# Split order of the summed weight blocks and plain fp32 first slices in a 64-sequence LoRA MLP with a per-sequence mix

## The chip, the cores and the metric

One core of one Trainium2 chip runs the kernel. The metric is the device time of one execution in microseconds (us). Before the change the median of 3 runs is 457.58 us (457.47 to 458.84).

## The reference

64 sequences of 32 rows with 512 features (2048 rows of `x`). Each group of sequences picks one of 16 adapters (`itok_B_2_6`) for the first step and one of 16 conditions (`itok_B_0_15`) for the second. All in float32:

```python
def lora_add(base, inp, A, B):
    t = jnp.einsum('bri,bni->bnr', A[0][idx], inp)          # rank 16
    return base + jnp.einsum('bor,bnr->bno', B[0][idx], t) * 0.5
gate = lora_add(x @ W_gate.T, x, A_gate, B_gate)            # 512 -> 1376
up   = lora_add(x @ W_up.T,   x, A_up,   B_up)
act  = silu(gate) * up
x    = x + lora_add(act @ W_down.T, act, A_down, B_down)    # 1376 -> 512
x    = x + einsum('bct,bcd->bdt', x, L1_weights[cond])      # mixes the 32 rows of a sequence
```

## The kernel before, in words

**Tiles and pairs.** Four sequences make a tile of 128 rows, 16 tiles make 8 pairs. The first phase (pairs 0 to 7) computes gate and up, with `xT` (features x rows) as the stationary operand and the weights as the moving one; the result is turned, written to `actT_dram` ("spilled") and read back by the second phase, which runs tile by tile (`down`, 16 times) over 11 chunks of `W_down` and ends each tile with the mix of the tile before it.

**Three products for one.** Every fp32 operand is split into a high fp32r part, copied by ACT (`hi`, L500), and the rest, subtracted by DVE (`lo`, L763; for the adapters' B rows L767). TensorE then runs hi x hi, hi x lo and lo x hi, three matmuls per 128-feature slice. So the order is always landing, ACT, DVE, TensorE, and each weight is split once.

**Sections and blocks.** The 1376 columns stand in three sections of 352, 512 and 512; a unit `k` is a section and a tile of the pair, k = 0 to 5. Pairs 0 and 1 (`plain_pair`) compute everything directly (`base`, L1151). From pair 2 on (`fast_pair`) sections 1 and 2 are done with one Winograd step over 2x2 blocks: the weight blocks b11, b12, b21, b22 give the summed blocks t1 to t4 (`sum_weights`, DVE, L793 to L802), which are then split (`split_forms`, `SPLITS` L51), and the pair's two `xT` tiles give sums in place (`sum_x`), split into `s_hi`, `s_lo` (`split_s`). The seven products on TensorE in a fast pair (L1231 to L1269) are called here P1 (b11), P7 (t3, the second sum), P2 (b21), P6 (t2), P5 (t1), P4 (t4), P3 (b22); each is 6 matmuls for gate and 6 for up, 512 columns wide. ACT copies P1 (`copy_p1`) and P7 (`copy_p7`), DVE adds them in (`add_u3`, `add_u7`).

**The work around them.** Per tile TensorE also computes the adapters' rank part (`lora`, 4 matmuls); its B rows arrive by a gather that POOL issues into `b_raw` as soon as DVE has split the last ones (`gather_b`, L448). SP issues, in a fixed order in each pair (L348): the next pair's `xT` (waits until `split_s` has read the old one, `s_ready`, L321), the last section's spill, the next pair's A rows (`load_a`, L386, 8 DMAs), and two spills. ACT's and DVE's order is written out by hand (L588 to L643, L887 to L964). Every engine runs its list in order, so an instruction that waits holds up all that is behind it.

**Which waits matter below.** `base(pr, 0)` waits until unit 3 of the pair before is gated (L1166), P1 until unit 0 is gated (L1235), `lora` on `b_ready` and `tT_ready`. In the second phase `down(1, 1)` waits until all of pair 7 is gated (L1402). DVE's list there: pair 7's units 4 and 5 are gated (L1100, L1102), then tile 1's `actT` is split, then the adapter part of tile 0 is masked (`mask_td`, which waits for the end of `down(0, 0)`). SP spills pair 7's last section (L416) ahead of the loads of `actT` for tiles 2 and 3 (L417, L418).

**The start.** TensorE's first matmul waits for the split first slices of `xT` and of the gate weights (L1157, L1141).

## Time and profile before

| | before |
|---|---|
| median of 3 runs | 457.58 us |
| profiled execution, its own time | 457.48 us |
| its span (first to last instruction) | 455.6 us |
| mean granted TensorE clock | 0.996 |
| busy: PE, DVE, ACT, POOL | 437.4, 335.0, 213.3, 168.2 us |
| PE idle before its first matmul | 5.25 us |
| PE idle from the end of its last matmul | about 2.7 us |

The profiled execution took 457.48 us, 1.9 us more than its span, and 0.1 us less than the median. Instruction rows give start (us from the span's start), duration, engine, line, operation, what is written and read, and in brackets how long the engine had been idle and what released it. A matmul's duration holds its fill; back to back, the distance between two starts is what it costs. "fp32r" results are the split parts.

### The profile page before, as it was taken

The numbers are of one execution on the slowest core, as the hardware profiler recorded it, in microseconds if no ns is written. First come the engines' busy times: TensorE is split into PE (matmuls) and PEld (weight loads), VectorE is DVE, ScalarE is ACT, GpSimd is POOL, SyncE is SP. The second block draws the span as 40 slices with busy tenths as digits, with TensorE's granted clock in tenths as the row PEclk, the third lists the DMA queues.
The fourth block names the chain that finished last, engine by engine and source line by source line (L and its number), as shares of the span: only waits on it lengthen the run. The fifth ranks groups of instructions, "written<-read, shape, count | busy, mean of one in ns | idle before, by whom it ended". The sixth has DMA issues, their size and how long they took to land.

```text
span 455.6 us, 7248 instructions
## 1 busy us (share of the span) xinstructions
PE 437.4 (96%) x2465; PEld 393.9 (86%) x2465; DVE 335.0 (74%) x621; ACT 213.3 (47%) x396; POOL 168.2 (37%) x156
## 2 busy tenths in 40 slices
PE   5999999977999999999999999988999999999997
PEld 4978988865898888888888888988999999999996
DVE  6778698876876866967867857976766676676665
ACT  6664334365436335444444444925434545433441
POOL 3612120120311211111111551675566676665630
PEclk9999999999899999999999999999999999999999
DMA  8965663325667467466475589787556666555631
GB/s 268 378 221 150 182 181 108 104 81 147 167 170 210 109 163 193 112 199 157 112 205 148 141 260 337 196 201 201 170 173 192 205 199 202 176 175 175 201 104 46
DMA packets 99699, 81.12 MB, mean 178 GB/s; under 512 B 50928, under 2 KB 83056, under 8 KB 99664
## 3 DMA queue, kind: packets, MB, share of 16 engines
q1 hardware_dynamic: 88368, 47.27, 37.1%
q0 software_dynamic: 11008, 33.30, 24.0%
q8 instruction: 19, 0.31, 0.3%
q10 hardware_dynamic: 288, 0.10, 0.1%
q14 instruction: 16, 0.13, 0.1%
HBM read 65.18 MB, written 15.47 MB: 177 GB/s over the span
## 4 chain that ended last, share of the span: by engine, by line
PE 86%; DVE 7%; DMA 2%; ACT 2%; issue 1%; SPq 1%; DVEq 0%; ACTq 0%
PE bank L1300 24%; PE bank L1146 9%; PE bank L1147 9%; PE bank L1148 8%; PE bank L1191 8%; PE bank L1192 8%; PE bank L1193 8%; PE bank L1214 4%; PE bank L1213 4%; PE bank L1330 2%; DVE wd L763 2%; DMA actT_raw<-actT_dram 2%; PE bank L1310 1%; DVE b_gu L767 1%; PE bank L1315 1%
## 5 line engine op out<-in xcount | busy, mean ns | idle before, releaser
L441 POOL DMA_INDIRECT b_raw<-in_b_rows,rows x48 | 50.8, 1059 | 199.3 <-DVE b_gu L767 198.7
L1300 PE MATMUL bank<-wd,actT_hi 128*128 128x288 f32 x648 | 112.0, 295 | 3.1 <-DVE actT_lo L763 1.9
L1300 PEld LDWEIGHTS bank<-wd,actT_hi 128*128 128x128 f32 x648 | 95.5, 188 | 4.7 <-issue 3.5
L441 POOL DMA_INDIRECT a_dn_raw<-in_a_dn_rows,rows x64 | 75.5, 1180 | 19.5 <-issue 19.5
L767 DVE SCALAR_TENSOR_TENSOR b_gu<-b_raw,low_rows,b_gu 128x1024 fp32r<-128x1024 f32 (+1 forms) x48 | 55.6, 1159 | 30.6 <-ACT b_gu L500 30.6
L1300 PE MATMUL bank<-wd,actT_lo 128*128 128x288 f32 (+1 forms) x324 | 69.4, 296 | 0.0
L1300 PEld LDWEIGHTS bank<-wd,actT_lo 128*128 128x128 f32 (+1 forms) x324 | 51.9, 188 | 0.0
L500 ACT ACTIVATE b_gu<-b_raw 128x1024 fp32r<-128x1024 f32 (+1 forms) x48 | 46.2, 963 | 12.2 <-DMA b_raw<-in_b_rows,rows 10.7
L585 ACT ACTIVATE act<-bank 128x512 f32<-128x512 f32 (+1 forms) x48 | 26.2, 547 | 44.1 <-PE bank L1214 43.9
L763 DVE TENSOR_TENSOR actT_lo<-actT_raw,actT_hi 128x1280 fp32r<-128x1280 f32 (+1 forms) x32 | 27.0, 885 | 15.5 <-ACT actT_hi L500 14.6
L872 DVE TENSOR_TENSOR act<-act,bank 128x512 f32<-128x512 f32 (+1 forms) x48 | 29.9, 622 | 8.1 <-PE bank L1214 7.3
L1213 PE MATMUL bank<-b_gu,tT_hi 128*128 128x512 f32 (+1 forms) x96 | 35.5, 370 | 0.0
L1214 PE MATMUL bank<-b_gu,tT_lo 128*128 128x512 f32 (+1 forms) x96 | 35.5, 370 | 0.0
L880 DVE STREAM_TRANSPOSE staging<-act 128x512 f32<-128x512 f32 (+1 forms) x48 | 31.4, 654 | 3.4
L500 ACT ACTIVATE tdT_hi<-tdT_raw 128x128 fp32r<-128x128 f32 x16 | 5.0, 311 | 60.2 <-DVE tdT_raw L1050 60.2
L1146 PE MATMUL bank<-w_gate_hi,xT_hi 128*128 128x480 f32 (+2 forms) x72 | 27.0, 375 | 5.5 <-DVE w_gate_lo L763 5.5
L441 POOL DMA_INDIRECT b_dn_raw<-in_b_dn_rows,rows x16 | 18.0, 1125 | 36.7 <-PE bank L1300 26.6
L1147 PE MATMUL bank<-w_gate_lo,xT_hi 128*128 128x480 f32 (+2 forms) x72 | 26.7, 371 | 0.0
L1148 PE MATMUL bank<-w_gate_hi,xT_lo 128*128 128x480 f32 (+2 forms) x72 | 26.7, 370 | 0.0
L500 ACT ACTIVATE actT_hi<-actT_raw 128x1280 fp32r<-128x1280 f32 (+1 forms) x32 | 23.3, 775 | 2.9 <-DMA actT_raw<-actT_dram 2.9
L1146 PEld LDWEIGHTS bank<-w_gate_hi,xT_hi 128*128 128x128 f32 x72 | 14.0, 195 | 8.3 <-issue 5.2
L1146 PE MATMUL bank<-w_up_hi,xT_hi 128*128 128x352 f32 x64 | 21.2, 331 | 0.0
(177 smaller groups left out, 993.8 us busy)
## 6 DMA issues: line engine op xcount, KB each, us to landing
actT_raw<-actT_dram SPq DMA_DIRECT2D x16, 640.0 KB
actT_dram<-staging SPq DMA_DIRECT2D x64, 128.0 KB, 2.8
x_sb<-in_x SPq DMA_DIRECT2D x16, 256.0 KB, 2.9
xT_raw<-in_xT SPq DMA_DIRECT2D x15, 256.0 KB, 3.0
out<-out_sb SPq DMA_DIRECT2D x15, 256.0 KB, 2.0
a_raw<-in_a_gu_rows SPq DMA_DIRECT2D x56, 64.0 KB, 2.4
actT_dram<-staging SPq DMA_DIRECT2D x32, 88.0 KB, 3.1
wd_raw<-in_w_down SPq DMA_DIRECT2D x10, 256.0 KB, 7.1
```

Of the source, the lines that this page charges most:

```text
L441: return pool.indirect_dma_start(dst, None, src, bass.IndirectOffsetOnAxis(ap=rows[:, tile, col:col + 1], axis=0))
L500: return nc.scalar.activation(dst, src, ACT.Copy)
L767: return nc.vector.scalar_tensor_tensor(b, raw, low_rows[:, :], b.bitcast(F32), ALU.mult, ALU.subtract)
L1146: pe.matmul(out_, x_hi, hi, start=(first and k == 0), stop=False)
L1147: pe.matmul(out_, x_hi, lo, start=False, stop=False)
L1148: last = pe.matmul(out_, x_lo, hi, start=False, stop=(stops and k == KH - 1))
L1191: pe.matmul(out_, xs[0], hi, start=(first and j == 0), stop=False, skip_group_check=True)
L1192: pe.matmul(out_, xs[0], lo, start=False, stop=False, skip_group_check=True)
L1193: last = pe.matmul(out_, xs[1], hi, start=False, stop=(j == 1), skip_group_check=True)
L1213: pe.matmul(out_, tT_hi[t][:, g, :], b, start=False, stop=False, skip_group_check=True)
L1214: pe.matmul(out_, tT_lo[t][:, g, :], b, start=False, stop=True, skip_group_check=True)\
L1300: last = pe.matmul(ps_down[e][half][:, 0:HALF], a[e][0:n, c, :], wd[0:n, c, part, at:at + HALF], start=(c == 0 and i == 0), stop=(c == NC ...
```

## The change

Four things are edited.

1. **The start** (`plain_slices`): the first tile's gate product of section 0 takes its first two 128-feature slices as one plain fp32 matmul each, on `xT_raw` and the landed weights, in place of three fp32r matmuls each. All splits stay, since tile 1 uses them. SP's reload of `xT_raw` also waits for these two.
2. **The weight sums and splits in pairs 0 to 2**: `sum_weights` works on one matrix at a time, the sums and `split_forms` are interleaved one by one from the end of pair 0 on, in the new order of `SPLITS`. In pair 2 only three of the eight splits are left (before: six). `s_hi[0]`, `s_lo[0]` move in SBUF so that they no longer share space with `t3_raw`; `split_s` is split into two halves with a count each, `s_of(0)` at the head of pair 2 and `s_of(1)` after the last t3 split. SP's loads of the next `xT` wait for their own half.
3. **TensorE in the fast pairs**: the wait for the B rows stands behind the product; in pair 2 the order P2, P7, P6 becomes P2, P6 gate, P7, P6 up.
4. **The change of phase**: `W_down` chunks are split one at a time in pair 7 (five instead of four of them there), tile 1's splits and `mask_td(0, 0)` go ahead of the gating of units 4 and 5, `down(1, 1)` waits for unit 3 only and begins with the high parts, the mix of tile 0 stands two chunks later, the A rows' split goes behind `residual_h` for two tiles, and SP issues `load_actT(2, 0)` ahead of pair 7's last spill.

```diff
--- the start (TensorE)
+            def plain_slices(out_):
+                for k in range(PLAIN_SLICES):
+                    pe.wait_ge(x_first_landed if k == 0 else xT_landed[0], 16)
+                    pe.wait_ge(gu_landed[k], 16)
+                    last = pe.matmul(out_, xT_raw[0][:, k * P:(k + 1) * P], landed_at(k), start=(k == 0), stop=False)
+                last.then_inc(x_plain_used, 1)
...
-                for k in range(KH):
+                if by_slice:
+                    plain_slices(out_)
+                for k in range(PLAIN_SLICES if by_slice else 0, KH):
...
-SPLITS = [(f, m) for f in ("t2", "t3", "t1", "t4") for m in MATRICES]
+SPLITS = [("t2", "gate"), ("t2", "up"), ("t1", "gate"), ("t1", "up"), ("t4", "gate"), ("t3", "gate"), ("t3", "up"),
+          ("t4", "up")]
...
-                    sp.wait_ge(s_ready, pr - PLAIN)
+                    sp.wait_ge(s_ready, 2 * (pr - PLAIN) - 1 + t)
...
             sp.wait_ge(s_used, FAST)
             load_x(0, 0)
+            load_actT(2, 0)
             load_x(1, 1)
             spill(PAIRS - 1, 2)
-            load_actT(2, 0)
             load_actT(3, 1)
--- ACT
-            def split_s(pr):
+            def split_s_of(pr, i):
                 sc.wait_ge(x_summed, 4 * (pr - PLAIN + 1))
                 reached(sc, s_used, pr - PLAIN)
-                if isinstance(pr, int) and pr == PLAIN:
-                    sc.wait_ge(w_ready, GU_PIECES + 4)
-                hi(s_hi[0][:, :], xT_raw[0][:, :])
-                hi(s_hi[1][:, :], xT_raw[1][:, :]).then_inc(s_hi_ready, 1)
+                if pr == PLAIN and i == 1:
+                    sc.wait_ge(w_ready, GU_PIECES + 7)
+                hi(s_hi[i][:, :], xT_raw[i][:, :]).then_inc(s_hi_ready, 1)
--- DVE, plain_pair(1)
-                sum_weights("t3")
+                sum_weights("t1", "up")
+                sum_weights("t2", "gate")
                 gating(pr, 0)
                 split_b(pr, 1, 0)
-                sum_weights("t1")
+                sum_weights("t2", "up")
...
--- TensorE, fast_pair
-                pe.wait_ge(b_ready[0], NS * pr + 2)
                 for i, m in enumerate(MATRICES):
                     pe.wait_ge(p1_copied, fast(pr, i))
                     p2 = product(ps[m][0][:, :], xT_hi[0], xT_lo[0], 1, "b21", m, False)
                     if i:
                         p2.then_inc(xT_used[0], 1)
+                    else:
+                        pe.wait_ge(b_ready[0], NS * pr + 2)
                     lora_half(ps[m][0][:, :], 0, i, PIECE)
                 if first:
+                    pe.wait_ge(s_ready, 1)
+                    pe.wait_ge(w_ready, GU_PIECES + 2)
+                    p6("gate")
                     p7(pr)
+                    p6("up")
...
-                pe.wait_ge(b_ready[1], NS * pr + 2)
+                if first:
+                    pe.wait_ge(w_ready, GU_PIECES + 8)
--- TensorE, second phase
-            down(0, 0, first=True)
-            pe.wait_ge(act_ready, NU * PAIRS)
-            down(1, 1)
+            down(0, 0, early=True)
+            pe.wait_ge(act_ready, NU * (PAIRS - 1) + 4)
+            down(1, 1, early=True)
```

TensorE in pair 2, the products around the second of its two waits: `t2`, `t3`, `t1`, `t4` are the summed weight blocks, `s_hi0` and `s_hi1` the halves of the summed `xT`. First a piece of the end of P2 to the start of P6 before (one row of each group of three repeats with lo):

```order
L1213 MATMUL bank3<-b_gu0,tT_hi0 128x512
L1214 MATMUL bank3<-b_gu0,tT_lo0 128x512
L1191 MATMUL bank2<-t3_gate_hi,s_hi1 128x512
L1192 MATMUL bank2<-t3_gate_lo,s_hi1 128x512
L1193 MATMUL bank2<-t3_gate_hi,s_lo1 128x512
...
L1191 MATMUL bank5<-t3_up_hi,s_hi1 128x512
...
L1191 MATMUL bank6<-t2_gate_hi,s_hi0 128x512
...
L1191 MATMUL bank7<-t2_up_hi,s_hi0 128x512
```

and the same place now:

```order
L1268 MATMUL bank3<-b_gu0,tT_hi0 128x512
L1269 MATMUL bank3<-b_gu0,tT_lo0 128x512
L1246 MATMUL bank6<-t2_gate_hi,s_hi0 128x512
L1247 MATMUL bank6<-t2_gate_lo,s_hi0 128x512
L1248 MATMUL bank6<-t2_gate_hi,s_lo0 128x512
...
L1246 MATMUL bank2<-t3_gate_hi,s_hi1 128x512
...
L1246 MATMUL bank5<-t3_up_hi,s_hi1 128x512
...
L1246 MATMUL bank7<-t2_up_hi,s_hi0 128x512
```

Behind P2 there now come P6 gate, both halves of P7 and P6 up, where P7 and P6 stood before.

DVE in pair 2, from `s_lo1` (now from the split of section 1's B rows for tile 0) to the B rows `b_gu1` of section 1 before and to the second addition of P7 (`bank3<-bank7`) now. Before:

```order
L763 TENSOR_TENSOR s_lo1<-xT_raw1,s_hi1 128x512
L872 TENSOR_TENSOR act1<-act1,bank4 128x352
L880 STREAM_TRANSPOSE staging0<-act1 128x11x32
L763 TENSOR_TENSOR t1_gate_lo<-gu_landing,t1_gate_hi 128x1024
L763 TENSOR_TENSOR t1_up_lo<-gu_landing,t1_up_hi 128x1024
L872 TENSOR_TENSOR act0<-act0,bank3 128x512
L840 TENSOR_TENSOR bank0<-bank6,e_sbgate 128x512
L840 TENSOR_TENSOR bank3<-bank7,e_sbup 128x512
L880 STREAM_TRANSPOSE staging1<-act0 128x16x32
L763 TENSOR_TENSOR t4_gate_lo<-gu_landing,t4_gate_hi 128x1024
L763 TENSOR_TENSOR t4_up_lo<-gu_landing,t4_up_hi 128x1024
L767 SCALAR_TENSOR_TENSOR b_gu1<-b_raw1,low_rows,b_gu1 128x1024
```

and now:

```order
L791 SCALAR_TENSOR_TENSOR b_gu0<-b_raw0,low_rows,b_gu0 128x1024
L787 TENSOR_TENSOR t3_up_lo<-t3_raw,t3_up_hi 128x1024
L787 TENSOR_TENSOR s_lo1<-xT_raw1,s_hi1 128x512
L898 TENSOR_TENSOR act1<-act1,bank4 128x352
L906 STREAM_TRANSPOSE staging0<-act1 128x11x32
L787 TENSOR_TENSOR t4_up_lo<-gu_landing,t4_up_hi 128x1024
L898 TENSOR_TENSOR act0<-act0,bank3 128x512
L791 SCALAR_TENSOR_TENSOR b_gu1<-b_raw1,low_rows,b_gu1 128x1024
L866 TENSOR_TENSOR bank0<-bank6,e_sbgate 128x512
L906 STREAM_TRANSPOSE staging1<-act0 128x16x32
L866 TENSOR_TENSOR bank3<-bank7,e_sbup 128x512
```

Four splits of 1024 columns (`t1` and `t4`) stood between `s_lo1` and the B rows `b_gu1` of 1024 columns; one is left, and those B rows are split ahead of the additions.

DVE at the change of phase, before, from the split of the last `W_down` chunk to `mask_td(0, 0)` (`t_dn`, `tdT`), with `act0` and `act1` the units 4 and 5 of pair 7:

```order
L763 TENSOR_TENSOR wd<-wd_raw,wd 96x512
L872 TENSOR_TENSOR act0<-act0,bank7 128x512
L880 STREAM_TRANSPOSE staging2<-act0 128x16x32
L763 TENSOR_TENSOR wd<-a_dn_raw1,wd 128x4x11x16
L872 TENSOR_TENSOR act1<-act1,bank5 128x512
L880 STREAM_TRANSPOSE staging2<-act1 128x16x32
L763 TENSOR_TENSOR actT_lo1<-actT_raw1,actT_hi1 128x1280
L763 TENSOR_TENSOR actT_lo1<-actT_raw1,actT_hi1 96x128
L767 SCALAR_TENSOR_TENSOR b_dn<-b_dn_raw0,low_rows,b_dn 128x512
L1045 TENSOR_TENSOR t_dn<-bank1,mask 128x128
L1050 STREAM_TRANSPOSE tdT_raw<-t_dn 128x128
```

and now:

```order
L787 TENSOR_TENSOR wd<-wd_raw,wd 96x512
L787 TENSOR_TENSOR wd<-a_dn_raw1,wd 128x4x11x16
L787 TENSOR_TENSOR actT_lo1<-actT_raw1,actT_hi1 128x1280
L787 TENSOR_TENSOR actT_lo1<-actT_raw1,actT_hi1 96x128
L791 SCALAR_TENSOR_TENSOR b_dn<-b_dn_raw0,low_rows,b_dn 128x512
L1084 TENSOR_TENSOR t_dn<-bank1,mask 128x128
L1089 STREAM_TRANSPOSE tdT_raw<-t_dn 128x128
L787 TENSOR_TENSOR tdT_lo<-tdT_raw,tdT_hi 128x128
L898 TENSOR_TENSOR act0<-act0,bank7 128x512
L906 STREAM_TRANSPOSE staging2<-act0 128x16x32
L898 TENSOR_TENSOR act1<-act1,bank5 128x512
L906 STREAM_TRANSPOSE staging2<-act1 128x16x32
```

The gating of both units moved behind the splits of tile 1 and behind `mask_td(0, 0)`.

## Rows read from the trace of the kernel before

**Rows 1.** Waits of PE, the costliest group: what, for whom, total us, times, longest us.

```profile
PE bank L1191 <- DVE b_gu L767: 5.7, 2, 3.4
```

**Rows 2.** Timeline of PE at the start, in pair 0.

```profile
6.75 0.66 PE L1146 MATMUL bank<-w_gate_hi,xT_hi 128*128 128x352 f32 x1 [0.28 <-DVE w_gate_lo L763]
...
26.00 0.33 PE L1146 MATMUL bank<-w_gate_hi,xT_hi 128*128 128x128 f32 x1
```

**Rows 3.** Timeline of ACT at the start.

```profile
4.05 0.50 ACT L500 ACTIVATE w_gate_hi<-gu_landing 128x352 fp32r<-128x352 f32 x1 [0.78 <-DMA gu_landing<-in_w_gate]
```

**Rows 4.** Timeline of DVE in the first tile's and second tile's work.

```profile
6.18 0.95 DVE L763 TENSOR_TENSOR w_gate_lo<-gu_landing,w_gate_hi 128x352 fp32r<-128x352 f32 x2
...
25.25 0.69 DVE L763 TENSOR_TENSOR w_gate_lo<-a_raw,w_gate_hi 128x512 fp32r<-128x512 f32 x1
```

**Rows 5.** Timeline of PE at the end: the one plain fp32 product.

```profile
452.17 0.75 PE L1345 MATMUL bank<-x_sb,last_mix_w 128*128 128x288 f32 x2 [0.17 <-DVE x_sb L1125]
```

**Rows 6.** Timeline of PE in pairs 2 and 3: P1, P2, P4, `base` and P1 of pair 3.

```profile
92.57 0.39 PE L1191 MATMUL bank<-b_gate_hi,xT_hi 128*128 128x512 f32 x1
92.80 0.40 PE L1192 MATMUL bank<-b_gate_lo,xT_hi 128*128 128x512 f32 x1
...
98.44 0.50 PE L1191 MATMUL bank<-b_gate_hi,xT_hi 128*128 128x512 f32 x1 [2.31 <-DVE b_gu L767]
...
113.96 0.61 PE L1191 MATMUL bank<-t_gate_hi,xT_hi 128*128 128x512 f32 x1 [3.43 <-DVE b_gu L767]
...
122.97 0.38 PE L1146 MATMUL bank<-w_gate_hi,xT_hi 128*128 128x480 f32 x1
...
133.59 0.39 PE L1191 MATMUL bank<-b_gate_hi,xT_hi 128*128 128x512 f32 x1
```

**Rows 7.** Busy time, granted clock, DMA share and GB/s of one stretch.

```profile
114.00:116.00 2.00, 2.00 (x5) 1.58 (x6) 2.00 (x4) 1.02 (x2) 1.15 (x1) 0.55 0.76 165
```

**Rows 8.** Timeline of DVE in pair 2.

```profile
91.08 0.48 DVE L872 TENSOR_TENSOR act<-act,bank 128x352 f32<-128x352 f32 x1
...
98.50 1.29 DVE L763 TENSOR_TENSOR s_lo<-xT_raw,s_hi 128x512 fp32r<-128x512 f32 x2
```

**Rows 9.** Timeline of SP's DMA issues.

```profile
99.82 0.83 SPq L322 DMA_DIRECT2D xT_raw<-in_xT  x2
...
104.50 8.58 SPq L389 DMA_DIRECT2D a_raw<-in_a_gu_rows  x8
```

**Rows 10.** Timeline of ACT, pair 2: the second tile's A rows.

```profile
114.55 0.63 ACT L500 ACTIVATE w_gate_hi<-a_raw 128x512 fp32r<-128x512 f32 x1 [0.17 <-DMA a_raw<-in_a_gu_rows]
```

**Rows 11.** Timeline of DVE, end of pair 3 and start of pair 4.

```profile
152.69 0.69 DVE L872 TENSOR_TENSOR act<-act,bank 128x512 f32<-128x512 f32 x1 [0.61 <-PE bank L1214]
...
161.97 0.94 DVE L767 SCALAR_TENSOR_TENSOR b_gu<-b_raw,low_rows,b_gu 128x704 fp32r<-128x704 f32 x1
...
165.19 0.48 DVE L872 TENSOR_TENSOR act<-act,bank 128x352 f32<-128x352 f32 x1
```

**Rows 12.** Timeline of PE at the change of phase.

```profile
300.15 0.77 PE L1300 MATMUL bank<-wd,actT_hi 128*128 128x288 f32 x4 [1.91 <-DVE actT_lo L763]
...
311.50 0.77 PE L1300 MATMUL bank<-wd,actT_hi 128*128 128x288 f32 x4 [1.20 <-issue]
...
321.98 0.70 PE L1300 MATMUL bank<-wd,actT_hi 128*128 128x288 f32 x4
```

**Rows 13.** Timeline of DVE at the change of phase.

```profile
300.58 0.28 DVE L1045 TENSOR_TENSOR t_dn<-bank,mask 128x128 f32<-128x128 f32 x1
...
304.05 0.75 DVE L1065 TENSOR_TENSOR x_sb<-x_sb,bank 128x224 f32<-128x224 f32 x2
304.89 0.88 DVE L763 TENSOR_TENSOR h_lo<-x_sb,h_hi 128x224 fp32r<-128x224 f32 x2
309.71 1.69 DVE L763 TENSOR_TENSOR actT_lo<-actT_raw,actT_hi 128x1280 fp32r<-128x1280 f32 x2 [3.94 <-ACT actT_hi L500]
```

**Rows 14.** The chain that ended last, 296 to 322 us: start, us, what.

```profile
301.31 6.87 DMA actT_raw<-actT_dram
```

More of the change, by code:

```diff
@@ L84, in build @@
             t3_raw = sb("t3_raw", [P, 2, 2 * PIECE], F32, ramp)
-        s_hi = [sb(f"s_hi{i}", [P, KH * P], F32R) for i in range(2)]
-        s_lo = [sb(f"s_lo{i}", [P, KH * P], F32R) for i in range(2)]
+        s_hi, s_lo = [None, None], [None, None]
+        s_hi[1] = sb("s_hi1", [P, KH * P], F32R)
+        s_lo[1] = sb("s_lo1", [P, KH * P], F32R)
         e_sb = [sb(f"e_sb{m}", [P, 512]) for m in MATRICES]
+        s_hi[0] = sb("s_hi0", [P, KH * P], F32R)
+        s_lo[0] = sb("s_lo0", [P, KH * P], F32R)
         act = [sb(f"act{i}", [P, 512]) for i in range(2)]
@@ L827, in sum_x, with split_s_of @@
                 nc.vector.tensor_tensor(a12, a12, a11, ALU.subtract).then_inc(x_summed, 1)
+            def split_s_of(pr, i):
+                ve.wait_ge(s_hi_ready, 2 * (pr - PLAIN) + i + 1)
+                lo(s_lo[i][:, :], xT_raw[i][:, :], s_hi[i][:, :]).then_inc(s_ready, 1)
             def split_s(pr):
-                ve.wait_ge(s_hi_ready, pr - PLAIN + 1)
-                lo(s_lo[0][:, :], xT_raw[0][:, :], s_hi[0][:, :])
-                lo(s_lo[1][:, :], xT_raw[1][:, :], s_hi[1][:, :]).then_inc(s_ready, 1)
+                for i in range(2):
+                    split_s_of(pr, i)
             def add_u3(pr, i):
@@ L1017, in _ @@
             split_b(0, 2, 1)
+            sum_weights("t3", "gate")
             split_x(1, 1)
             gating(0, 4)
+            sum_weights("t3", "up")
+            sum_weights("t1", "gate")
             split_b(1, 0, 0)
@@ L1078, in residual_out, with down @@
                 nc.vector.tensor_tensor(out_sb[e][:, :], x_sb[e][:, :], ps_mix[:, 0:H], ALU.add).then_inc(out_ready, 1)
-            def down(m, e, first=False, last=False):
-                if not first:
-                    mask_td(m - 1, 1 - e)
-                    split_mix(m - 1, 1 - e)
+            def down(m, e, last=False):
+                mask_td(m - 1, 1 - e)
+                split_mix(m - 1, 1 - e)
                 if not last:
                     split_a_dn(m + 1, 1 - e)
-                if not first:
-                    residual_h(m - 1, 1 - e)
+                residual_h(m - 1, 1 - e)
                 if not last:
@@ L1093, in down @@
                 split_b_dn(m, e)
-                if not first:
-                    residual_out(m - 1, 1 - e)
+                residual_out(m - 1, 1 - e)
             split_a_dn(0, 0)
             split_actT(0, 0)
-            split_down(4, NC)
+            split_down(5, NC)
+            split_a_dn(1, 1)
+            split_actT(1, 1)
+            split_b_dn(0, 0)
+            mask_td(0, 0)
             gating(PAIRS - 1, 4)
-            split_a_dn(1, 1)
             gating(PAIRS - 1, 5)
-            split_actT(1, 1)
-            ve.wait_ge(s_used, FAST)
-            split_b_dn(0, 0)
-            down(1, 1)
-            down(2, 0)
+            split_mix(0, 0)
+            residual_h(0, 0)
+            split_a_dn(2, 0)
+            split_actT(2, 0)
+            split_b_dn(1, 1)
+            residual_out(0, 0)
+            mask_td(1, 1)
+            split_mix(1, 1)
+            residual_h(1, 1)
+            split_a_dn(3, 1)
+            split_actT(3, 1)
+            split_b_dn(2, 0)
+            residual_out(1, 1)
             down(3, 1)
@@ L1155, in base @@
                 first = ramp and k == 0
-                if first:
-                    pe.wait_ge(x_first_ready, 1)
-                elif s == 0:
+                if s == 0 and not first:
                     pe.wait_ge(xT_ready[t], pr + 1)
```

178 lines of the change are left out of this document (106 added, 72 removed).

## The prediction

> **What bounds the kernel now.** I read the page first: TensorE (PE) is busy 437.4 of 455.6 us, and PE takes 86% of the chain that ended last. So time can come back only where PE waits or runs at the lower clock, and the second view is the list of PE's waits: two on the adapters' B rows, 5.7 us in sum and the longest 3.4, lead it [rows 1], beside 5.25 us before the first matmul. The third view, PE's timeline, places them: the B rows in pair 2, at 98.44 and 113.96 [rows 6], 1.91 and 1.20 us at the head of `down(1, 1)` and `down(2, 0)` for `actT` [rows 12]. The fourth, the granted clock, shows a further cost: after the longer wait the stretch 114 to 116 ran at 0.55 of full speed, PE's lower level of 1.2 GHz against 2.4 [rows 7]; after the 2.31 us wait it did not fall. Between pair 3 and pair 7 PE never waits, so what is gained in pair 2 stays gained, and what is lost there stays lost. Everything the change does elsewhere (waits behind the product instead of ahead of it, `s_ready` counted in halves) finds no PE wait to remove: nothing.
>
> **The start: nothing.** The first gate weights have landed by 4.05 [rows 3], so PE can begin at about 4.1 instead of 5.3. A plain fp32 matmul goes through as two records; 288 columns took 0.75 us [rows 5], where four fp32r matmuls of 288 columns together take 0.69 [rows 12]: about four times one fp32r matmul. At the lower clock of the start three fp32r matmuls of 352 columns need 0.9 us a slice, so I take 1.2 for a plain slice, with 0.75 and 1.8 (0.75 scaled to 352 columns, doubled for the clock) as bounds. Two end at 6.5; the third slice is split at 6.18 + 0.95 = 7.13 [rows 4] and starts at 7.2. Before, the second began at 6.75 [rows 2] and the third 0.9 later, at 7.65: PE is 0.45 us ahead (with 1.8 a slice 0.1 us behind). But at 26.00 PE starts the rank part of tile 1 [rows 2] right when DVE's split of its A rows ends, 25.25 + 0.69 [rows 4], and that row shows no idle worth a bracket: PE was there at most 0.2 us earlier. DVE's list up to there hangs on gathers and is not shortened. So the lead becomes a wait at 26.0. If the plain slices were slower than every bound, 0.2 us of cover is gone soon and the rest would show in full. Taken: 0, range -0.3 to +0.2.
>
> The Trainium skill ("TensorE: Matmul & The Clock Gate", part 1) says that the array is throttled by default and that activity releases it, so a new gap in the start could also hold the lower clock longer. By rows the start waits once now as before, for 0.3 us before and some 0.7 after, and the lead of 0.45 covers most of it; by the page half a microsecond might be lost once, which I do not add.
>
> **Pair 1: nothing.** The weight sums and five splits (DVE 1.2 us each, like the 1.23 of a 1024-column split; before: two) move into holes where DVE waited; in order I get the last `sum_x` at the time it had. PE's needs there have over 2 us of room. The tightest place is the head of pair 2: `s_of(0)` puts 0.7 us in front of the gating of unit 0, which stood at 91.08 + 0.48 [rows 8] and is now done at 92.3; P1 wants it at 92.57 [rows 6]. Room 0.3 us, cost 0 (0 to 0.3).
>
> **Pair 2: 5.3 us.** Back to back a 512-column matmul costs 92.80 - 92.57 = 0.23 us [rows 6]. From 92.57: P1 12 of them and 4 of 352 columns, to 96.0; P2 needs ACT's copy of P1 (ACT now splits `b_gu0` ahead of it, in time) and, behind the product, the B rows, split at about 96.4: no wait. P2 16, to 99.6; P6 gate, P7, P6 up 24, to 105.2; P5 12, P4 16, P3 16, to 115.3. What they wait for: the last t3 split ends at 98.3, `s_of(1)` at 99.65, before P7 at 101.0; the last t4 split at 101.9 and `b_gu1` at 103.8 are long before P4 at 107.9. The additions follow the products by what they do in later pairs. So `base(3, 0)` could start at 115.3 instead of 122.97 [rows 6], 7.7 us earlier: the two waits and the slow stretch.
>
> It cannot, because what is late next are the A rows of pair 3. SP issued the loads of pair 3's `xT` when both `s_lo` were done (98.50 + 1.29, issue at 99.82 [rows 8, 9]), then four spills, and the eight A loads from 104.50 over 8.58 us; ACT had the last at 114.55, still waiting for it [rows 9, 10]. Now `s_of(1)` ends at 99.65, one `xT` load is already out, so SP is 0.1 + 0.4 us earlier and the last A rows land at 114.0. ACT and DVE split them in 1.25 us; both have the gating of unit 3 behind that, so DVE gates it at 115.25 to 115.95, and `base(3, 0)` waits for it (L1166): 0.6 us. From there DVE has no hole: in pair 4 the same list ran from the gating of unit 3 at 152.69 to the end of the B rows at 161.97 + 0.94 and to the gating of unit 0 at 165.19 + 0.48 [rows 11], 10.2 and 13.0 us. From 115.25: B rows at 125.5, unit 0 at 128.25. PE's `lora(3, 0)` would be due 8.1 us after `base`, at 124.1, and waits 1.4; P1 follows at 128.3 instead of 133.59 [rows 6]: 5.3 us kept. Bounds: 7.7 if the A rows were no limit; each us by which they land later costs one. The last A load took 1.5 us (issued by 113.08, landed at 114.55); with the 6.87 us of `actT` [rows 14] only 0.1 would be left.
>
> A second page rule speaks against the term: the Trainium skill ("DMA: Bandwidth & Descriptors", the section that issuing engines are not separate DMA queues) says that DMAs of all issuers share the 16 DMA engines. Rows agree that the stretch is loaded: 0.76 DMA share in 114 to 116 [rows 7]. The gather of tile 1's B rows, which came after the A loads before, now runs at 104 to 106 beside them. By rows the term is 5.3, by the rule a little less; that is a rival below.
>
> **Change of phase: 3.5 us.** `down(0, 0)` keeps its place (DVE splits one chunk less ahead of it, PE has room). `down(1, 1)` needs only unit 3 and the high part of tile 1, which by my order is split by 294.7, so it starts when `down(0, 0)` ends, about 298.1, not 300.15 [rows 12]: 2.05. Then DVE's list: `mask_td(0, 0)` starts at 298.3, not 300.58 [rows 13], and takes 1.3; the gating of units 4 and 5 takes 4 steps of 0.7 (0.69 for one [rows 11]), to 302.5; the mix split 0.8; `residual_h` 304.05 to 305.77, so 1.7 [rows 13], to 305.0; the mix, two chunks later, is due at 305.8: 0.8 of room. A rows 0.8 and `actT` 1.69 [rows 13] more, with ACT's high part ahead of it by 306.7, so tile 2 is split at 308.4. Its load was behind the spill, 6.87 us in the air from 301.31 [rows 14], and is issued at 290 now; it is no longer what comes last. PE would be ready at 308.15 and starts `down(2, 0)` at 308.5 instead of 311.50 [rows 12]. `down(2, 0)` no longer has its 0.3 us wait for the mix, so `down(3, 1)` starts at 318.5 instead of 321.98: 3.5 us. Behind the late gating stands pair 7's last spill, 302.5 instead of 298.46, and `load_actT(3, 1)`; it lands at about 312 and is used at 314.5: room 2.5. Bounds: 2 (only the first wait goes) and 3.8 (no 0.3 us at `down(2, 0)`). Later tiles repeat without waits.
>
> **Sum.** 0 + 0 + 5.3 + 3.5 = 8.8 us. Span 455.6 - 8.8 = 446.8; profiled execution 457.48 - 8.8 = 448.7 (it stands 0.1 under the median of 457.58). Forecast 448.7.
>
> **Rivals.**
>
> *A, the opening of pair 3 gives more back* (chance 0.22). The A rows land 1 to 2 us later than 114.0 beside the gather, or the two short waits (0.6 and 1.4) bring the lower clock, as the 3.43 us one did; that fall cost 7.7 - 2.3 - 3.4 = 2.0 us, restarts included. For it: the loaded stretch; against: 2.31 us alone did not lower the clock. Time 449.8 to 452.
>
> *B, the A rows are no limit* (0.12). SP's four spills are issued earlier or the loads are faster, as in pair 4, where the second tile's were no limit. 7.7 + 3.5: 446.3.
>
> *C, the change of phase turns its waits into new ones* (0.12). `mask_td` and late gating stand in a row on DVE, and `residual_h` or tile 2's split come late by more than their 0.8 and -0.3 us; then only 2 or less is left: 450.2 to 452.
>
> *D, slower* (0.03). One mechanism: PE falls to the lower clock at pair 3's opening and its short waits keep it there. Work at that level costs as much again, so 8.8 us are used up from some 9 us of full-speed work on and all beyond is loss; one fast pair of 33 us at that level would end at about 480. Against: after the one fall of this trace the level came back soon, since the mean granted clock is 0.996.
>
> *E, the change does not do what it says* (0.03): a wait of pair 2 on another count takes the place of the one removed, for instance P7 on `s_of(1)`, which has 1.3 us of room. Within 0.3% if it eats all.
>
> **How the numbers follow.** The forecast's own case, 447.7 to 449.7, has 0.48. With A and C at the upper end and B at the lower the range that leaves under 2 in 10 out is 446.2 to 451.8. A run can tell 0.3% (1.4 us) from no change; faster by more than that needs under 456.2: all but D, E: 0.95. Within 0.3%: 0.02. Slower: 0.03.
>
> **What the profile will show.** No PE idle before P2, P4 in pair 2 and full clock from 100 to 120; `base(3, 0)` at about 116 behind DVE's gating, and a wait of about 1.4 us on the B rows before `lora(3, 0)`; ACT idle on the last A rows at about 114. The first matmul at 4.1 and a wait at 26.0. `down(1, 1)` without a wait, a small one at `down(2, 0)` on `actT`. I am wrong if `base(3, 0)` starts before 115.6 or after 117.5, if the 26.0 start moves, or if the mix of tile 0 waits.

## The result, and the profile after

| | before | changed |
|---|---|---|
| median (runs) | 458.21 us (4; 457.47 to 460.0) | 451.9 us (4; 451.15 to 453.57) |
| ratio to before | | 0.9862, 95% interval 0.982 to 0.9904 |
| profiled execution, span | 457.48, 455.6 us | 452.14, 450.3 us |
| busy: PE, DVE, ACT | 437.4, 335.0, 213.3 us | 438.5, 335.2, 213.3 us |

The forecast was 448.7 us (446.2 to 451.8). The time is 3.2 us above it and just outside the range; the gain is 6.3 us by the medians and 5.3 by the two spans, where 8.8 were forecast. The median of before has moved from 457.58 to 458.21 us because a fourth execution (460.0) joined the three. Three marks show in which stretch it is missing. Mark 1 is the matmul of section 2 in pair 0 that waits some 0.8 us for DVE's gating, mark 2 is P1 of pair 3, mark 3 the first matmul of `down(3, 1)`; behind mark 3 both kernels take 133.6 us.

| us | mark 1 | 1 to 2 | 2 to 3 | sum |
|---|---|---|---|---|
| before | 33.33 | 100.26 | 188.39 | 321.98 |
| changed | 34.45 | 96.17 | 186.04 | 316.66 |
| difference | +1.12 | -4.09 | -2.35 | -5.32 |
| forecast | 0 | -5.3 | -3.5 | -8.8 |

Every stretch gave 1.1 or 1.2 us less than forecast. The waits of PE in the changed kernel (what, for whom, total us, times, longest us):

```profile
PE bank L1189 <- DMA gu_landing<-in_w_gate: 4.4, 2, 4.1
PE bank L1203 <- DVE act L898: 2.7, 2, 2.0
PE bank L1367 <- issue: 1.4, 2, 1.1
```

The two waits for the B rows, 5.7 us in sum [rows 1], are gone. In their place stand 2.0 us for DVE's gating, and 1.4 us of "issue", for nothing that the profile shows. That label alone does not prove that nothing was waited for: before's 1.20 us at `down(2, 0)` has it too [rows 12], and there the program does wait for `actT`. Here it is the program that has no wait at the place, as shown below.

**The start.** Timeline of PE:

```profile
4.08 1.51 PE L1189 MATMUL bank<-gu_landing,xT_raw 128*128 128x352 f32 x2 [4.08 <-DMA gu_landing<-in_w_gate]
5.88 1.51 PE L1189 MATMUL bank<-gu_landing,xT_raw 128*128 128x352 f32 x2 [0.29 <-DMA gu_landing<-in_w_gate]
7.93 0.66 PE L1203 MATMUL bank<-w_gate_hi,xT_hi 128*128 128x352 f32 x1 [0.55 <-DVE w_gate_lo L787]
...
27.11 0.33 PE L1203 MATMUL bank<-w_gate_hi,xT_hi 128*128 128x128 f32 x1
```

PE begins at 4.1 as forecast and a plain slice takes 1.5 us, inside the bounds of 0.75 and 1.8. But the second slice waits for its weights, which landed later, and tile 1's rank part begins at 27.11, not at 26.00 [rows 2]. That is right when DVE's split of tile 1's A rows ends, 26.37 + 0.69, as the prediction had it; but DVE's list itself is 1.1 us later. The rest of the first `xT` came 0.75 us later than before (ACT splits it at 5.27, idle for it):

```profile
5.27 0.52 ACT L506 ACTIVATE xT_hi<-xT_raw 128x384 fp32r<-128x384 f32 x1 [0.80 <-DMA xT_raw<-in_xT]
```

```profile
26.37 0.69 DVE L787 TENSOR_TENSOR w_gate_lo<-a_raw,w_gate_hi 128x512 fp32r<-128x512 f32 x1
```

What the prediction and e1 call the lower clock of the start is read from the pace of the matmuls (352 columns every 0.29 us up to 13.7, every 0.16 after). The granted clock of the profile reads 1.00 all through 0 to 14 us, in before too.

**Pair 2.** PE, from the end of P3 on, then ACT, which waits for the A rows:

```profile
118.31 0.45 PE L1203 MATMUL bank<-w_gate_hi,xT_hi 128*128 128x480 f32 x1 [2.00 <-DVE act L898]
...
130.62 0.39 PE L1246 MATMUL bank<-b_gate_hi,xT_hi 128*128 128x512 f32 x1
```

```profile
116.22 0.63 ACT L506 ACTIVATE w_gate_hi<-a_raw 128x512 fp32r<-128x512 f32 x1 [4.46 <-DMA a_raw<-in_a_gu_rows]
```

P2 and P4 wait no more. `base(3, 0)`, the 480-column row at 118.31, waits behind DVE's gating, as the text had it, but for 2.0 us and not 0.6, since the last A rows are there at 116.22; counted from mark 1 that is 1.1 us later than forecast. And the clock falls after this wait, from 119.7 on and for some 3.4 us, and there is no wait before `lora(3, 0)`, where 1.4 us were forecast. Busy time of PE, PEld, DVE, ACT, POOL, then granted clock, DMA share and GB/s:

```profile
118.00:120.00 2.00, 1.69 (x7) 1.53 (x8) 1.89 (x4) 1.29 (x2) 0.00 (x0) 0.93 0.06 15
120.00:122.00 2.00, 2.00 (x6) 1.65 (x5) 1.93 (x4) 0.00 (x0) 0.95 (x1) 0.50 0.95 205
122.00:124.00 2.00, 2.00 (x10) 1.94 (x9) 1.86 (x5) 1.50 (x3) 0.00 (x0) 0.72 0.85 212
```

**Change of phase.** PE, from the mix of tile 0 in `down(1, 1)` to `down(2, 0)`, and DVE:

```profile
303.24 0.40 PE L1384 MATMUL bank<-h_lo,mix_hi 128*128 128x512 f32 x1
303.47 0.43 PE L1367 MATMUL bank<-wd,actT_hi 128*128 128x288 f32 x2
304.12 0.29 PE L1367 MATMUL bank<-wd,actT_hi 128*128 128x288 f32 x1 [0.23 <-issue]
305.55 0.30 PE L1367 MATMUL bank<-wd,actT_hi 128*128 128x288 f32 x1 [1.13 <-issue]
305.68 0.42 PE L1367 MATMUL bank<-wd,actT_lo 128*128 128x288 f32 x2
305.94 0.70 PE L1367 MATMUL bank<-wd,actT_hi 96*128 96x288 f32 x4
306.48 0.42 PE L1367 MATMUL bank<-wd,actT_lo 96*128 96x288 f32 x2
306.74 0.69 PE L1367 MATMUL bank<-wd,actT_hi 128*128 128x288 f32 x4
```

```profile
303.43 1.69 DVE L787 TENSOR_TENSOR actT_lo<-actT_raw,actT_hi 128x1280 fp32r<-128x1280 f32 x2 [0.47 <-ACT actT_hi L506]
```

Both waits of before, 1.91 and 1.20 us [rows 12], are gone, and the mix does not wait. But PE stands still in the middle of chunk 9: of four matmuls in a row, on the same operands and with no wait between them in the program, the third and the fourth start late. By the starts the four should take 0.53 us and took 2.21, 1.7 us too long. The profile calls 1.36 us of that idle, and the idle time is what is called the pause below. In marks 2 to 3 it costs 1.3, by the same kernel without it (e5).

### The profile page after: what moved, and what is told of

It is laid out like the page before. It is cut to its first block, busy times and chain, and to the rows that moved or that the text cites. A ratio compares the mean times of both kernels' runs of the same rounds, so it can differ in the third digit from the quotient of the medians.

```text
span 450.3 us, 7219 instructions
## 1 busy us (share of the span) xinstructions
PE 438.5 (97%) x2463; PEld 394.3 (88%) x2463; DVE 335.2 (74%) x621; ACT 213.3 (47%) x396; POOL 170.0 (38%) x156
## 4 chain that ended last, share of the span: by engine, by line
PE 91%; SPq 2%; DVE 2%; issue 1%; ACT 1%; DMA 1%; ACTq 0%
PE bank L1367 28%; PE bank L1203 9%; PE bank L1204 9%; PE bank L1205 9%; PE bank L1247 7%; PE bank L1248 7%; PE bank L1246 7%; PE bank L1268 4%; PE bank L1269 4%; PE bank L1397 2%; PE bank L1377 2%; SPq L347 1%; DMA xT_raw<-in_xT 1%; PE bank L1382 1%; PE bank L1383 1%
## 5 line engine op out<-in xcount | busy, mean ns | idle before, releaser
L1367 PE MATMUL bank<-wd,actT_hi 128*128 128x288 f32 (+1 forms) x636 | 110.2, 295 | 1.4 <-issue 1.4
L1367 PEld LDWEIGHTS bank<-wd,actT_hi 128*128 128x128 f32 (+1 forms) x636 | 93.8, 188 | 2.3 <-issue 1.1
L447 POOL DMA_INDIRECT a_dn_raw<-in_a_dn_rows,rows x64 | 77.5, 1212 | 19.5 <-issue 19.5
L1367 PE MATMUL bank<-wd,actT_lo 128*128 128x288 f32 (+1 forms) x318 | 68.1, 296 | 0.0
L506 ACT ACTIVATE b_gu<-b_raw 128x1024 fp32r<-128x1024 f32 (+1 forms) x48 | 46.2, 963 | 10.5 <-DMA b_raw<-in_b_rows,rows 8.8
L447 POOL DMA_INDIRECT b_dn_raw<-in_b_dn_rows,rows x16 | 15.8, 990 | 35.0 <-PE bank L1367 24.1
L506 ACT ACTIVATE h_hi<-x_sb 128x224 fp32r<-128x224 f32 (+1 forms) x30 | 11.1, 414 | 22.8 <-DVE x_sb L1104 22.8
```

The costliest lines, as they stand in the source:

```text
L447: return pool.indirect_dma_start(dst, None, src, bass.IndirectOffsetOnAxis(ap=rows[:, tile, col:col + 1], axis=0))
L506: return nc.scalar.activation(dst, src, ACT.Copy)
L1367: last = pe.matmul(ps_down[e][half][:, 0:HALF], a[e][0:n, c, :], wd[0:n, c, part, at:at + HALF], start=(c == 0 and i == 0), stop=(c == NC ...
```

## The experiments

Sixteen runs, some of them repeats of one kernel, came in four sets, each set on one chip beside runs of the kernel before, whose median there was 458.44, 457.52, 458.82 and 457.42 us. The changed kernel's own median in the second and fourth set was 450.31 and 450.14. Numbers in brackets behind a median say how far it is below before's in its set. Every run has one profile, of one of its executions, so marks and waits are those of that one.

### Set 1: the start, the A rows, the change of phase

**e1, the start of before.** `x_first_ready` and the wait for it are back, `plain_slices` is gone:

```
-                for k in range(PLAIN_SLICES if by_slice else 0, KH):
+                for k in range(KH):
```

> The changed kernel with the start of before: all four slices of the first product split in high and low, PE waits for DVE's first low part, no plain fp32 matmul. Theory S (the two plain slices themselves cost what the start lost): the first matmul at 5.3, the granted clock rises at about 11.7 instead of 13.8, the rank part of tile 1 starts at 26.0 instead of 27.11, span 450.3 - 1.1 = 449.2 and median 450.8. Rival D (the second xT load landed 0.75 us later in that run by chance and everything after hangs on it): no difference that can be told from zero, median 451.9, and the landing of xT differs from run to run without regard to the start.

Measured: 451.64 us (-6.8), span 450.9, mark 1 at 33.58. The tile's rest of `xT` was at ACT at 4.52. That alone would look like theory S. But e4, with the same start, had it at 5.44 and mark 1 at 34.54, and e2, with plain slices, had mark 1 at 33.25. Over all profiles mark 1 lies between 33.25 and 34.68 in 13 kernels with plain slices (mean 34.09), and between 33.33 and 35.18 in 5 with split ones, before's own among them (mean 34.11). Rival D holds: with values that scatter by 1.4 and 1.9 us no worth of the start can be told from zero, and its time goes with when loads land. (By the medians of e2 and e4, which differ in the start alone, plain slices would be 0.9 us the faster, within the scatter of their six executions each.) The first profile of before has nearly the earliest start of all, so every sum made against it asks for 0.8 us too much.

**e2, the A loads early.**

```
                 load_xT(pr + 1, 0)
+                if early:              # pair 2
+                    spill(pr - 1, 2)
+                    load_a(pr + 1, 0)
+                    load_a(pr + 1, 1)
                 load_xT(pr + 1, 1)
```

> The changed kernel with one edit: in pair 2, SP issues pair 1's last spill and the eight loads of pair 3's A rows between the two xT loads, so the A loads are issued from about 94 instead of 106.4. Theory A (the A rows are what base(3, 0) waits for): base(3, 0) starts at 116.2 right behind P3, without its 2.0 us wait and without the fall of the granted clock at 120; DVE gates unit 3 at 113.5 to 115 instead of 117.5, so its list of 10.2 and 12.9 us ends 2.4 to 3.8 us earlier and P1 of pair 3 starts at 126.8 to 128.2 instead of 130.62: median 448.1 to 449.5. Rival B (DVE's list of pair 3 hangs on the gathered B rows or on the clock, not on the A rows): the wait at base(3, 0) goes but comes back before lora(3, 0), P1 of pair 3 stays at 130 to 131, median 451.9.

Measured: 448.05 us (-10.4), in the range of theory A. ACT has both tiles' A rows in one go, without waiting:

```profile
105.77 1.14 ACT L512 ACTIVATE w_gate_hi<-a_raw 128x512 fp32r<-128x512 f32 x2
```

PE never waits between 34 and 298 us, and from mark 1 to P1 of pair 3 it takes 92.32 us: 3.9 less than in the changed kernel, 7.9 less than before. So the whole 7.7 us that I had worked out for pair 2 are there; the A rows are what withheld them, and PE meets no further limit behind. The profile has the pause, 1.41 us of idle time in chunk 9.

**e3, the change of phase of before.** `down(1, 1)` waits for all of pair 7 again, the lists of ACT, DVE and SP at the change of phase are before's:

```
-            pe.wait_ge(act_ready, NU * (PAIRS - 1) + 4)
-            down(1, 1, early=True)
+            pe.wait_ge(act_ready, NU * PAIRS)
+            down(1, 1)
```

> The changed kernel with the change of phase of before: down(1, 1) waits for all of pair 7's gating and for both parts of tile 1, mix after chunk 7, the gating of units 4 and 5 and the load of tile 2 in their old places. Theory (my term of the prediction): 3.5 us are lost, 1.9 at the head of down(1, 1), 1.2 at down(2, 0), 0.3 at its mix: median 455.4. By the profile of the changed kernel only 2.35 were gained there, since PE paused 1.4 us in the middle of chunk 9 of down(1, 1) with no wait in the program: then median 454.2 if the pause stays away here. Rival (the pause belongs to the place in the instruction stream, not to the early down(1, 1)): the pause shows here too, near 305, and the difference is again 3.5.

Measured: 452.91 us (-5.5), marks 2 to 3 187.60. The difference to the changed kernel is 1 to 1.6 us, less than either expectation (3.5, or 2.3 without the pause). Against the changed kernel without the pause (e5, 184.77) it is 2.8. Its waits were 1.89, 0.43 and 0.16 us, where before had 1.91 and 1.20 for the first two [rows 12], and it had no pause, which the others had.

**e4, both.**

> Both edits together: the start of before (all slices split) and the A loads of pair 3 ahead. If theories S and A hold, their gains lie in different stretches and add up: 451.9 - 1.1 - (2.4 to 3.8) = 447.0 to 448.4. If only A holds 448.1 to 449.5; if only S 450.8; if neither 451.9.

Measured: 448.96 us (-9.5), marks 1 to 2 again 92.36; only A holds. Marks 2 to 3 are 187.3, 1.2 more than in e2, and 0.76 of that is a wait for DVE at P5 of pair 7 that e2 does not have; why it came here is open. Here the pause is spread over three matmuls:

```profile
301.55 0.29 PE L1363 MATMUL bank<-wd,actT_hi 128*128 128x288 f32 x1 [0.44 <-issue]
302.28 0.29 PE L1363 MATMUL bank<-wd,actT_hi 128*128 128x288 f32 x1 [0.43 <-issue]
302.99 0.40 PE L1363 MATMUL bank<-wd,actT_hi 128*128 128x288 f32 x1 [0.42 <-issue]
```

### Set 2: the pause

**e5, the changed kernel again.**

> The changed kernel itself once more, on the chip of the runs beside it. It gives the time that the edits around it are compared with, 451.9 if the first measurement was typical, and a second look at three places. By both theories of the start its landing of xT may differ by up to 1 us from the first profile. Theory G (the fall of the granted clock comes with the wait of 2.0 us at base(3, 0)): fall and wait again together. The pause of 1.3 to 1.45 us in chunk 9 of down(1, 1), seen in all four kernels with the early down(1, 1), is there again.

Measured: 450.31 us (-7.2), interval of the ratio 0.9816 to 0.9851. The pause is not there. PE, same place:

```profile
302.66 0.40 PE L1384 MATMUL bank<-h_lo,mix_hi 128*128 128x512 f32 x1
302.90 0.70 PE L1367 MATMUL bank<-wd,actT_hi 128*128 128x288 f32 x4
303.43 0.43 PE L1367 MATMUL bank<-wd,actT_lo 128*128 128x288 f32 x2
303.70 0.69 PE L1367 MATMUL bank<-wd,actT_hi 96*128 96x288 f32 x4
304.23 0.43 PE L1367 MATMUL bank<-wd,actT_lo 96*128 96x288 f32 x2
304.65 0.76 PE L1367 MATMUL bank<-wd,actT_hi 128*128 128x288 f32 x4
```

The same program with the same neighbours (DVE's split of tile 2 again 0.04 us ahead of chunk 9) runs through, and `down(2, 0)` waits 0.16 us for `actT` (forecast 0.35). `lora(3, 0)` waits 1.13 us for the B rows (forecast 1.4). Marks 2 to 3 are 184.77, a gain of 3.6. Theory G is open: here `base(3, 0)` waited 1.80 us and the clock stayed at 1.00, in e1 too, in e3 it waited 2.00 and the clock fell; but before's wait of 2.31 us did not lower it in any of the three profiles that have it (before, e9, e14).

**e6, e7 and e8** take the kernel of e2. They were to tell what the pause hangs on. e6 repeats a small matmul 24 times ahead of P1 in pair 3, e7 has `mix_at = NC - 1`, e8 moves `split_actT(2, 0)` on DVE behind `residual_out(0, 0)`.

> The kernel with the early A loads, and in pair 3, ahead of P1, 24 more matmuls of 128 columns that write where the first of P1 then starts over (each a weight load and a matmul, so PE's stream of instructions is 48 longer from there). Theory F (the pause in down(1, 1) belongs to a place in PE's instruction stream, where the next instructions arrive late): the pause moves 24 matmuls or so to the front in the program, from chunk 9 into chunks 5 to 8 of down(1, 1). Rival V (it belongs to what the other engines do at that time: VectorE's split of tile 2's actT begins 0.03 us ahead of chunk 9 in all four): it stays at the third or fourth matmul of chunk 9. By both the time grows by about 1.5 to 2.5 us.

> The kernel with the early A loads, and the mix of tile 0 moved from after chunk 8 to after chunk 9 of down(1, 1) (of tile -1, none, in down(0, 0)). Chunk 9 now begins 0.7 us earlier, ahead of VectorE's split of tile 2's actT. Theory V (the pause begins with that split): chunk 9 runs at its pitch, and the pause comes in the mix or in chunk 10. Theory F (a place in the stream): the instruction at which it falls is three matmuls later in the program by the count, so at the end of chunk 9 or at the mix, with about the same time lost. A third reading, M (the first matmuls behind the mix are held by something of the mix): the pause is in chunk 10, right behind the mix. Time 448.0 for all three unless the pause goes: then 446.7.

> The kernel with the early A loads, and VectorE's split of tile 2's actT moved behind the split of tile 1's B rows and the residual sum of tile 0, so it starts about 2 us later than chunk 9. Theory V: chunk 9 of down(1, 1) has no pause. Theory F: the pause is where it was, at the third and fourth matmul of chunk 9. By both a wait is added at the head of down(2, 0), 0 to 1.7 us, since its operand comes later: by V it then starts about 0.3 us later than now, by F the pause hides the delay in part and it starts 0.3 to 1 us later.

Measured: 449.38 (-8.1), 447.06 (-10.5) and 449.07 us (-8.5). None has a pause, but nor has e5, so none of the three tells F, V and M apart; what they add is that the early A loads give marks 1 to 2 of 92.32 again (e7, e8), and e8 its wait of 1.78 us at `down(2, 0)`, the delay of the split in full.

### Set 3: the terms apart, and the gather

Set 3 ran on the chip of set 1.

**e9, before with the change of phase alone.**

> The kernel before with the change of phase alone (the early down(1, 1), the late gating of units 4 and 5, mix after chunk 8, the load of tile 2 ahead of the last spill, the chunks' splits spread). My term: from P1 of pair 3 to down(3, 1) 3.5 us less than before's 188.4, so 184.9, and 3.5 us off the median of before. In the first profile of the changed kernel it was 186.0 with a pause of 1.4 us in chunk 9 of down(1, 1), in the second 184.6 without it. Theory X (the pause is not the program's, it comes with the chip or the moment): this kernel gives 184.6 to 185 without a pause or 186 with one, and its sister in this set with the early A loads, which paused 1.41 us on another chip, does the same here as this one. Rival: the pause belongs to the kernel with the early A loads wherever it runs.

Measured: 455.25 us (-3.6), marks 2 to 3 184.69. The term of 3.5 us is right in full where no pause falls in it. PE at the head of `down(2, 0)`, with before's 1.20 [rows 12] down to 0.17:

```profile
308.28 0.43 PE L1320 MATMUL bank<-wd,actT_lo 96*128 96x288 f32 x2
308.71 0.76 PE L1320 MATMUL bank<-wd,actT_hi 128*128 128x288 f32 x4
```

**e10, the gather behind the A rows.**

```
                 reached(pool, b_ready[t], NS * pr + s)
+                if (pr, s, t) == (PLAIN + 1, 0, 0):
+                    pool.wait_ge(a_hi_ready[1], PLAIN + 2)
```

> The changed kernel, and GpSimd's gather of tile 0's B rows for pair 3, which ran at 111.0 to 112.1 beside the last A loads, waits until ScalarE has the last A rows. Theory Q (the gather delays the A rows; they landed 2.2 to 3.0 us after the issue of the last load, in before 1.5): now 1.5, so the last A rows at ScalarE 0.7 to 1.4 us earlier, base(3, 0) 0.7 to 1.4 earlier after a wait of about 0.6 to 1.1 us, P1 of pair 3 0.7 to 1.4 earlier. Rival W (the eight spills issued right behind the A loads take their place): no change of more than 0.3 us. The gathered rows are needed at about 123 and land at about 121.

**e11, the spills behind the A rows.**

```
+                    if s == 0 and isinstance(pr, int) and pr == PLAIN:
+                        sp.wait_ge(a_hi_ready[1], PLAIN + 2)
                     spill(pr, s)
```

> The changed kernel, and SyncE's spills of pair 2's first two sections, which were issued from 112.8 right behind the A loads, wait until ScalarE has the last A rows. Rival W: the last A rows land 1.5 us after their issue, 0.7 to 1.4 us earlier than in the changed kernel. Theory Q: they land as before the edit, 2.2 to 3.0 us after it. By both the load of pair 4's xT is issued at about 124 to 125 as now, since eight spills take 8 us, and no more than 0.5 us is lost behind.

Measured: e10 448.89 us (-9.9), e11 450.64 us (-8.2; marks 1 to 2 95.22, 2 to 3 185.60, with a wait of 0.52 us at P5 of pair 7, the place of e4's). SP, ACT and POOL of e10:

```profile
104.55 8.06 SPq L395 DMA_DIRECT2D a_raw<-in_a_gu_rows  x8
```

```profile
113.99 0.63 ACT L508 ACTIVATE w_gate_hi<-a_raw 128x512 fp32r<-128x512 f32 x1 [3.55 <-DMA a_raw<-in_a_gu_rows]
```

```profile
104.84 0.94 POOL L447 DMA_INDIRECT b_raw<-in_b_rows,rows  x1 [6.68 <-DVE b_gu L793]
115.41 0.95 POOL L447 DMA_INDIRECT b_raw<-in_b_rows,rows  x1 [9.63 <-ACT w_gate_hi L508]
```

And the same three of e5, the unedited kernel:

```profile
104.32 8.44 SPq L395 DMA_DIRECT2D a_raw<-in_a_gu_rows  x8
```

```profile
115.73 0.63 ACT L506 ACTIVATE w_gate_hi<-a_raw 128x512 fp32r<-128x512 f32 x1 [5.21 <-DMA a_raw<-in_a_gu_rows]
```

```profile
104.88 0.94 POOL L447 DMA_INDIRECT b_raw<-in_b_rows,rows  x1 [6.68 <-DVE b_gu L791]
110.97 1.16 POOL L447 DMA_INDIRECT b_raw<-in_b_rows,rows  x1 [5.15 <-DVE b_gu L791]
```

From the issue of the last A load to ACT's use of it: 112.61 to 113.99 = 1.4 us with the gather moved away, 112.76 to 115.73 = 3.0 with it at 111. The table has all profiles with the A loads in their place:

| gather in 110 to 113? | last load to use, us |
|---|---|
| no: before, e9, e14 | 1.5, 1.5, 1.5 |
| no: e10, e15 | 1.4, 1.5 |
| yes: changed, e1, e3, e5, e13 | 2.2, 2.5, 2.8, 3.0, 2.4 |
| yes, spills later: e11 | 2.6 |

Theory Q holds: the load took 1.4 to 1.5 us in all five profiles without the gather and 2.2 to 3.0 in the six with it, and moving the gather away brings it back. W is worth at most a few tenths. `base(3, 0)` of e10 starts at 116.09 after no wait worth a bracket, and P1 of pair 3 at 128.21.

**e12, the early A loads again.**

> The kernel with the early A loads once more, on another chip. Theory X: the pause in chunk 9 of down(1, 1), 1.41 us the first time, is there or not together with the other kernels of this set; without it the time is 1.4 us lower against before than the first time, so a difference of 11.8 us to the median of before instead of 10.4. Rival: the pause is there again, difference 10.4, whatever the others do.

Measured: 446.62 us (-12.2; ratio 0.9736, interval 0.9711 to 0.9762), no pause. It is the kernel of e2 on the chip of e2.

### Set 4: does it come back?

> The changed kernel a third time. Theory X (the pause in chunk 9 of down(1, 1) comes with the chip or the moment, not with the program): all four kernels of this set pause there, or none; without it this kernel is 7.0 to 7.5 us under before, with it 5.8 to 6.3. Rival Y (it comes at random in each execution): some of the four pause and some don't.

> The kernel before with the change of phase alone, a second time. From P1 of pair 3 to down(3, 1) 184.7 us without the pause, 186.0 with it; by X as the three others of this set. Its time 3.6 us under before without, 2.2 with the pause.

> The changed kernel with the gather behind the last A rows, a second time. Theory Q: last A rows at ScalarE 1.3 to 1.7 us after the issue of their last load, in the changed kernel beside it 2.2 to 3.0; P1 of pair 3 1.2 to 1.8 us earlier than there, and the time 1.2 to 1.8 us lower. Rival: the 1.75 us of the first time were chance, and the two kernels of this set are within 0.5 us of each other.

> The kernel with the early A loads, a third time, for the difference to the changed kernel on one chip: P1 of pair 3 is 3.3 to 4.2 us earlier, its start counted out, and the time 3.3 to 4.2 us lower. By X its pause goes with the three others'.

Measured: e13 450.14 (-7.3), e14 456.1 (-1.3), e15 449.05 (-8.4), e16 447.68 us (-9.7). No pause in any, so by the one profile of each kernel sets go as one (X), three without and one with it. Marks 2 to 3 of these kernels come back to 0.05 us. Marks 1 to 2 come back to 0.1 where no A load is waited for, and differ by 0.3 and 0.7 where one is:

| us | mark 1 | 1 to 2 | 2 to 3 |
|---|---|---|---|
| e9, e14 phase only | 33.90, 35.18 | 100.20, 100.32 | 184.69, 184.69 |
| e5, e13 changed | 34.18, 34.43 | 95.78, 95.44 | 184.77, 184.79 |
| e10, e15 gather late | 34.14, 33.83 | 94.07, 94.78 | 184.75, 184.80 |
| e12, e16 A loads early | 34.34, 34.01 | 92.31, 92.31 | 184.64, 184.69 |

e15 beside e13 is 1.1 us faster, just short of the 1.2 to 1.8 that Q asked; by marks 1 to 2 the late gather gives 0.7 here (1.7 in e10 against e5), since e13's last load took 2.4 us and e5's 3.0. e16 beside e13 is 2.5 us faster where 3.3 to 4.2 were expected; by marks 1 to 2 it is 3.1, and its median is that of two executions, 446.53 and 448.84. e14's gain is 2.3 us smaller than e9's, though the marks behind the start are the same: its profile has the latest start of all, 35.18, and in 5 of its 8 executions (it still has before's two long waits) the mean clock was 0.992, in e9's in 1 of 4. Before's own nine executions of this set lie between 456.70 and 460.03, so a difference of medians can be off by a microsecond.

## Why the prediction was off by 3.2 us, point by point

- **What bounds it** was right: PE's waits and what they do to its clock. In all 36 executions of the kernel before in the four sets the mean granted clock is 0.988 to 0.996; in e5 and e13, without the long waits, it is 1.000 in 7 of 7 (in the first four of the changed kernel 0.996 twice and 1.000 twice). One fall as in the profile, 3.4 us at 0.50, takes 0.004 off the mean, so by this estimate 0.996 stands for one fall, 0.992 for two and 0.988 for three. The 16 executions of before at 0.996 took 457.6 us on average, the 17 at 0.991 to 0.993 took 458.7 and the three at 0.988 and 0.989 took 460.1. So the profile of before, with one fall, shows less of this cost than most executions pay.
- **The start, 0:** right as a mean (34.09 against 34.11), and the cover that I named is real: e12, whose PE was early, waits 1.1 us for the A rows at 26.91. That single profiles differ by up to 1.9 us (mark 1 from 33.25 to 35.18) I did not allow for. The 1.12 us of the first comparison are this; my test "wrong if the 26.0 start moves" was a bad one, since it moves by itself.
- **Pair 1, 0, and P1 of pair 2:** right; in pair 2 of the changed kernel no product waits.
- **Pair 2, 5.3:** measured 4.1, 4.5 and 4.8. The step that failed is the price of the last A load: "the last A load took 1.5 us", read from before, where no gather ran at that time. With the gather beside it, which my text noted only as coming at 104 to 106 (there is a second one at 111), it takes 2.2 to 3.0. That was rival A's mechanism, with chance 0.22. With the gather moved away the term is 6.2 and 5.5, with the A rows as no limit at all 7.9 (rival B had 7.7). The Trainium skill ("DMA: Bandwidth & Descriptors", the section that issuing engines are not separate DMA queues) says that DMAs of all issuers share the 16 DMA engines. The traces agree in that POOL's gather delays SP's load: e10 against e5 makes it 1.6 us on one load, e15 against e13 0.9.
- **How late the A rows were:** in the profile of the changed kernel the price of that load is 0.7 of 1.1 us; the rest is that SP was through with its issues 0.3 us later than forecast. In e5 the load took 1.5 us more and the issues were 0.7 us early. `base(3, 0)` started at 118.31, behind the 117.5 that I had named as a sign of being wrong (117.2 with mark 1's delay taken off). That the 451.9 lies in rival A's range, 449.8 to 452, is in part luck, since the pause is in it; but the 450.3 and 450.1 without the pause lie in it too.
- **The fall of the clock** at `base(3, 0)`, the other half of rival A, cost little: from the gating of unit 3 to P1 it took 13.13 us with it (117.49 to 130.62) and 12.96 without (117.00 to 129.96 in e5). DVE's list set the end of that stretch, as forecast (13.0), so what PE lost in it was hidden.
- **Change of phase, 3.5:** right, 3.6 to 3.75 in the nine profiles without the pause whose kernels add or delay nothing in this stretch and that have no wait in pair 7 (e11, which has one, gave 2.8). With the pause, 2.35. No row of the profile of before could have told of it.
- **The level:** 0.6 us of the miss is before's median, 457.58 from three runs at the forecast and 458.21 with a fourth. This overlaps with the start: both say that the profile of before was a fast one.

By size: the pause 1.3, the A rows 0.5 to 1.2, the level 0.6, the start up to 1.1 in that profile; they overlap and add up to more than the 3.2. In the two later sets the changed kernel ran at 450.3 and 450.1 us, 7.2 and 7.3 under before: the error left there is 1.5 us, the A rows and the early start of the profile against which the sum was made.

**Open:** what the pause is. It is no wait of the program. The place, the order on DVE or the chip is not enough for it, since the same kernel ran with and without it (the changed kernel and e5; e2 and e12, these two on the same chip). But all four pauses fell among the first four matmuls behind the mix, with DVE's split of tile 2 just begun, so that place or order has no part in it is not shown. It was in all profiles of the early `down(1, 1)` up to e4, and in none of the twelve after, one execution each. In e1 the clock fell behind it as well (0.50 in 306 to 308), which makes marks 2 to 3 187.84 there.

**The better version** is that of e2, e12 and e16: the A loads early, 10.4, 12.2 and 9.7 us under before. Beside the changed kernel on one chip it is 2.5 us faster (e16 and e13), and with the mix one chunk later 3.3 (e7 and e5).
